# Turning quantised activations by DMA instead of on TensorE, in a fused sequence layer

## The chip, the cores and the metric

The kernel runs on one core of a Trainium2 chip. The metric is the device time of one execution in microseconds (us); lower is better. The engines are named as in the profile: PE (TensorE) with its weight loads PEld, DVE (VectorE), ACT (ScalarE), POOL (GpSimd) and SP (SyncE), which only issues DMAs. Each engine runs its own instructions in order and waits for others through semaphores.

## The reference, cut to what matters

The input x has 8 sequences of 512 rows of 256 values.

```
v      = x @ W_write.T
reads  = chunked decaying linear attention of x over itself, values v
x1     = layernorm(x + x + alpha * (reads @ W_read.T))
xq     = fp4(x1)                       # blocks of 16 along the row
gate   = xq @ fp4(w_gate).T            # 704 columns
up     = xq @ fp4(w_up).T
h      = silu(gate) * up
out    = layernorm(x1 + fp4(h) @ fp4(w_down).T)

fp4(a): scale = max(|block|) / 6 (at least 1e-12); a / scale is rounded to the
        grid 0, 0.5, 1, 1.5, 2, 3, 4, 6 with its sign, and multiplied by scale
```

## The kernel before, in words

The work is cut by sequence n (0 to 7), each of four tiles of 128 rows. Tiles of the second part are numbered k = 4n + t, 0 to 31. Buffers of two parities serve k, and pairs of tiles u = 0, 1 serve x. The 512 scores of a sequence are computed directly (the recurrence is folded into a decay mask). Float32 products are made of float32r parts: every operand is split into a rounded part (`_hi`) and a remainder (`_lo`), and a product is three matmuls (hi hi, hi lo, lo hi; `split_matmuls` L1709, `late_matmuls` L1719).

For a sequence: `scores` and `values` on PE from the transposed x; `decay_scores` on DVE (L1135); `reads` on PE; `x_residual` on DVE (L1159); the layernorm on ACT, DVE and POOL. Then x is quantised in pairs of tiles: maxima, scales and reciprocals on DVE; `x_normalise` on POOL (L390); squares on ACT (L680, into `x_sq`, bfloat16 in SBUF); `magic_add` (L1094) and `to_grid` (L1099) on DVE, which round to the grid by adding a large number; and `x_dequant` on POOL (L398), which multiplies the grid by its scale. PE transposes the result (`xq_transpose`, L1783), ACT rounds it (L688) and DVE takes the remainder (L1200).

For a tile k: `gate_up` on PE (512 + 512 + 384 columns, 18 matmuls) into three PSUM banks; silu on ACT (L699); the product on DVE (L1209); the same quantising of the 704 columns of h (L1215, L1083, L1084, L1089, L406, L703, L1094, L1099, L413); six transposes on PE (`h_transpose`, L1817), since the 704 columns are padded to 768 by repeating the last 64 (L712); rounding on ACT (L719) and the remainder on DVE in two parts (L1236); 17 matmuls of `down` (L1821); residual (L1245), deviations (L723) and layernorm (L731).

The four weights' parts in six pieces w are quantised the same way in the first 60 us and transposed by PE in nine fills.

The order on each engine is written out by hand as lists of calls: a prologue, a loop body of four tiles run three times, and an epilogue. Each call carries in its last argument the semaphores that say when its PSUM bank is free. SP loads x, x transposed and the weights, and stores 32 tiles of the output, in one list.

Of the kernel before, what the change touches and what calls it, by code (L numbers as in the profile page):

```python
# [5 lines left out]
F32 = mybir.dt.float32  # L31
F32R = mybir.dt.float32r
# [20 lines left out]
def mk_seq_postln_kernel(nc, x_rows, xt_rows, w_attn, w_ffn, scalars, out):  # L53
# [12 lines left out]
    PAIR = 2 * D  # L66
    WU = 6
# [4 lines left out]
    with ExitStack() as ctx:  # L72
# [3 lines left out]
        def sem(name):  # L76
# [36 lines left out]
        z_off = sb("z_off", [P, TILES, D], BF16)  # L113
# [7 lines left out]
        x_ns = sb("x_ns", [P, 2, 2 * XB + 2])  # L121
        x_rs = sb("x_rs", [P, 2, 2 * XB])
        x_n = sb("x_n", [P, 2, PAIR])
        x_sq = sb("x_sq", [P, 2, PAIR], BF16)
        x_y = sb("x_y", [P, 2, PAIR])
        x_g = sb("x_g", [P, 2, PAIR])
        x_q = sb("x_q", [P, TILES, D])
        xqT_hi = sb("xqT_hi", [P, DK, T], F32R)
        xqT_lo = sb("xqT_lo", [P, DK, T], F32R)
# [3 lines left out]
        h_am = sb("h_am", [P, 2, HB // 4, 5])  # L133
        h_sc = sb("h_sc", [P, 2, HB])
        h_ns = sb("h_ns", [P, 2, HB])
        h_rs = sb("h_rs", [P, 2, HB])
        h_n = sb("h_n", [P, 2, I])
        h_sq = sb("h_sq", [P, 2, I], BF16)
        h_y = sb("h_y", [P, 2, I])
        h_g = sb("h_g", [P, 2, I])  # L140
# [44 lines left out]
        v_left = sem("v_left")  # L185
# [3 lines left out]
        read_filled, z_ready, z_dev, z_var, z_rstd_ready, z_shift_ready = (  # L189
            sem("read_filled"), sem("z_ready"), sem("z_dev"), sem("z_var"), sem("z_rstd_ready"), sem("z_shift_ready"))  # L190
# [3 lines left out]
        xq_left = sem("xq_left")  # L194
        xqT_filled, xqT_hi_ready, xqT_lo_ready = sem("xqT_filled"), sem("xqT_hi_ready"), sem("xqT_lo_ready")
# [60 lines left out]
        def _(sp):  # L256
# [24 lines left out]

            load_x_transposed(1)
# [1832 lines left out]
```

## Time and profile before

| | |
|---|---|
| median of 3 runs | 324.37 us (324.2 to 324.91) |
| profiled execution, span | 322.5 us |
| time around the span, against the median | 1.9 us |
| PE busy | 314.5 us, 97% |
| PEld busy | 285.2 us, 88% |
| DVE busy | 293.0 us, 91% |
| POOL busy | 238.2 us, 74% |
| ACT busy | 213.2 us, 66% |
| DMA moved | 15.69 MB |

Busy time is the union of an engine's instructions. Matmuls overlap, so the mean of one instruction is its latency; how far apart they start is its cost. An instruction group's idle time stands only for the time just before it, with the engine that ended it.

### The profile page before, as it was taken

What the parts mean: (1) busy time and instruction counts of PE and PEld (TensorE: products, weight loads), DVE (VectorE), ACT (ScalarE), POOL (GpSimd) and SP (SyncE); (2) the same over time, 40 slices, a digit from 0 to 9 for tenths busy, and PEclk for the clock granted to TensorE, in tenths of its full rate; (3) what the DMA queues carried; (4) which work ended last, traced back from release to release, by engine and by line L of the source; (5) the groups of instructions that cost most, each with busy time, mean ns of one, the idle gap of its engine ahead of it and who ended that gap; (6) DMA issues with size and microseconds to landing.
All of it is one profiled execution on the core that took longest, in us unless ns stands there. A gap on an engine that the chain in (4) does not pass through costs nothing.

```text
span 322.5 us, 6519 instructions
## 1 busy us (share of the span) xinstructions
PE 314.5 (97%) x2067; PEld 285.2 (88%) x2067; DVE 293.0 (91%) x746; ACT 213.2 (66%) x521; POOL 238.2 (74%) x258
## 2 busy tenths in 40 slices
PE   7999999999999999999999999999999999999994
PEld 3999988989998998999989998898989889998983
DVE  4799789989899999899998999889999999999973
ACT  7769994767775647844784556766675555665664
POOL 1999898668696868676886768777779588368872
PEclk9999999999999999999999999999999999999999
DMA  6830301010010200320020200021000000001002
GB/s 227 302 125 9 132 0 67 1 66 2 1 67 16 84 16 0 100 82 3 16 83 17 83 17 3 33 65 35 1 18 17 16 18 17 19 16 35 17 33 84
DMA packets 8242, 15.69 MB, mean 49 GB/s; under 512 B 1040, under 2 KB 5136, under 8 KB 8208
## 3 DMA queue, kind: packets, MB, share of 16 engines
q1 hardware_dynamic: 7920, 15.01, 14.0%
q8 instruction: 17, 0.28, 0.4%
q10 hardware_dynamic: 288, 0.26, 0.3%
q14 instruction: 17, 0.14, 0.1%
HBM read 11.08 MB, written 4.19 MB: 47 GB/s over the span
## 4 chain that ended last, share of the span: by engine, by line
PE 69%; DVE 17%; issue 5%; ACT 4%; POOL 3%; ACTq 0%; DVEq 0%; POOLq 0%
PE gu L1712 11%; PE gu L1716 11%; PE gu L1713 11%; PE bank L1817 5%; PE bank L1712 4%; PE bank L1716 4%; PE bank L1713 4%; PE bank L1722 3%; DVE h_y L1094 3%; PE bank L1725 3%; PE bank L1726 3%; DVE w_raw L1209 2%; DVE hqT_lo L1236 2%; DVE h_am L1215 2%; PE bank L1783 2%
## 5 line engine op out<-in xcount | busy, mean ns | idle before, releaser
L413 POOL TENSOR_TENSOR h_q<-h_g,h_ns 128x704 f32<-128x704 f32 x32 | 51.2, 1604 | 47.7 <-DVE h_g L1099 47.6
L1712 PE MATMUL gu<-guT_hi,xqT_hi 128*128 128x512 f32 (+1 forms) x192 | 74.0, 386 | 0.7 <-DVE w_raw L1209 0.6
L1713 PE MATMUL gu<-guT_lo,xqT_hi 128*128 128x512 f32 (+1 forms) x192 | 72.2, 376 | 0.0
L1716 PE MATMUL gu<-guT_hi,xqT_lo 128*128 128x512 f32 (+1 forms) x192 | 56.6, 376 | 0.0
L699 ACT ACTIVATE w_raw<-gu 128x512 f32<-128x512 f32 x64 | 29.3, 462 | 32.7 <-PE gu L1716 32.4
L406 POOL TENSOR_TENSOR h_n<-w_raw,h_rs 128x704 f32<-128x704 f32 x32 | 47.0, 1472 | 3.4 <-DVE h_rs L1089 3.2
L719 ACT CAST hqT_hi<-bank 128x512 fp32r<-128x512 f32 x64 | 30.4, 478 | 17.7 <-PE bank L1817 17.2
L1712 PEld LDWEIGHTS gu<-guT_hi,xqT_hi 128*128 128x128 f32 x192 | 36.1, 188 | 6.0 <-ACT xqT_hi L688 0.9
L1716 PEld LDWEIGHTS gu<-guT_hi,xqT_lo 128*128 128x128 f32 x192 | 35.5, 188 | 6.0 <-ACT xqT_lo L693 0.2
L1713 PEld LDWEIGHTS gu<-guT_lo,xqT_hi 128*128 128x128 f32 x192 | 36.1, 188 | 4.8
L1094 DVE SCALAR_TENSOR_TENSOR h_y<-h_sq,h_n 128x704 f32<-128x704 bf16 x34 | 36.9, 1090 | 0.0
L1236 DVE TENSOR_TENSOR hqT_lo<-bank,hqT_hi 128x512 fp32r<-128x512 f32 x64 | 34.4, 542 | 1.9 <-ACT hqT_hi L719 1.8
L1209 DVE TENSOR_TENSOR w_raw<-w_raw,gu 128x512 f32<-128x512 f32 x64 | 32.4, 507 | 3.2 <-ACT w_raw L699 2.0
L1099 DVE SCALAR_TENSOR_TENSOR h_g<-h_sq,h_y 128x704 f32<-128x704 bf16 x34 | 32.4, 960 | 0.4
L368 POOL TENSOR_TENSOR pr_lo<-pr,pr_hi 128x512 fp32r<-128x512 f32 (+3 forms) x32 | 32.4, 1023 | 0.3 <-ACT pr_hi L658 0.3
L1817 PE MATMUL bank<-ident,h_q 128*128 128x128 f32 x192 | 30.4, 273 | 0.7 <-DVE wq_gu L1245 0.4
L1215 DVE TENSOR_REDUCE h_am<-w_raw 128x44 f32<-128x704 f32 x32 | 27.8, 868 | 0.3
L703 ACT ACTIVATE h_sq<-h_n 128x704 bf16<-128x704 f32 x32 | 25.4, 793 | 2.9 <-POOL h_n L406 2.9
L1817 PEld LDWEIGHTS bank<-ident,h_q 128*128 128x128 f32 x192 | 23.2, 140 | 4.5 <-issue 0.8
L398 POOL TENSOR_TENSOR x_q<-x_g,x_ns 128x512 f32<-128x512 f32 x16 | 18.3, 1142 | 11.7 <-DVE x_g L1099 11.7
L658 ACT CAST pr_hi<-pr 128x512 fp32r<-128x512 f32 (+3 forms) x32 | 14.7, 458 | 11.0 <-DVE pr L1135 10.9
L420 POOL TENSOR_TENSOR o_rstd<-o_ve,neg_half 128x1 f32<-128x1 f32 x31 | 19.5, 631 | 2.6 <-DVE o_ve L1252 2.6
(159 smaller groups left out, 936.7 us busy)
## 6 DMA issues: line engine op xcount, KB each, us to landing
xs<-in_x_rows_dram SPq DMA_DIRECT2D x8, 512.0 KB, 3.4
out_dram<-wq_gu SPq DMA_DIRECT2D x32, 128.0 KB, 1.7
x_full<-in_xt_rows_dram SPq DMA_DIRECT2D x7, 512.0 KB, 3.2
w_raw<-in_w_ffn_dram SPq DMA_DIRECT2D x6, 352.0 KB, 6.0
w_pair<-in_w_attn_dram SPq DMA_DIRECT2D x1, 512.0 KB, 5.2
x_full<-in_xt_rows_dram SPq DMA_DIRECT2D x1, 256.0 KB, 2.6
x_full<-in_xt_rows_dram ACTq DMA_DIRECT2D x1, 256.0 KB, 3.4
scal<-in_scalars_dram ACTq DMA_DIRECT2D x1, 1.0 KB, 1.7
```

The costliest lines, as they stand in the source:

```text
L368: nc.gpsimd.tensor_tensor(pr_lo[:, c], pr[:, c], pr_hi[:, c].bitcast(F32), ALU.subtract).then_inc(pr_lo_ready, 1)
L406: nc.gpsimd.tensor_tensor(blocks(h_n[:, p, :]), blocks(h[:, p, :]), per_block(h_rs[:, p, :], HB), ALU.mult).then_inc(h_norm, 1)
L413: nc.gpsimd.tensor_tensor(blocks(h_q[:, p, 0:I]), blocks(h_g[:, p, :]), per_block(h_ns[:, p, :], HB), ALU.mult).then_inc(h_quant, 1)
L1094: nc.vector.scalar_tensor_tensor(y, sq, MAGIC_C, v, ALU.add, ALU.add).then_inc(magic_sem, 1)
L1099: nc.vector.scalar_tensor_tensor(g, sq, MAGIC_C, y, ALU.add, ALU.subtract).then_inc(grid_sem, 1)
L1209: nc.vector.tensor_tensor(h[:, p, c], silu[:, p, c], up_of[half], ALU.mult).then_inc(h_ready, 1)
L1215: nc.vector.tensor_reduce(h_am[:, p, :, 0:4], blocks(h[:, p, :]), AX.X, ALU.max, apply_absolute_value=True).then_inc(h_amax, 1)
L1236: nc.vector.tensor_tensor(hqT_lo[:, p, c], h_bank[t][g][:, 0:c.stop - c.start], hqT_hi[:, p, c].bitcast(F32), ALU.subtract).then_inc(hT_lo ...
L1712: nc.tensor.matmul(dst, lh, rh, start=(first and i == 0), stop=False)
L1713: nc.tensor.matmul(dst, lh, rl, start=False, stop=False)
L1716: last = nc.tensor.matmul(dst, ll, rh, start=False, stop=(end and i == len(terms) - 1))
L1817: last = nc.tensor.transpose(h_bank[t][g][:, at - h_part[g].start:at - h_part[g].start + P], h_q[:, t % 2, at:at + P], ident[:])
```

## The change

The new kernel computes the same. Six things differ.

1. The grid of x and of h (multiples of a half up to 6) is written by `to_grid` as bfloat16 and turned by a transposing DMA from SBUF to SBUF (`turn_x_grid`, `turn_h_grid`). For h the repeated 64 columns are copied in the grid (`hg_repeat`).
2. The scales are transposed by PE in one instruction per tile of h or pair of x (`h_scale_rows`, `x_scale_rows`, 48 or 32 rows of 128), copied by ACT to SBUF, written to scratch in device memory by one DMA, and read back with every row repeated over the 16 partitions of its block (`spread_*`, 393 KB for h). So that the rows of one partition group lie together in scratch, `h_divisors` writes the scales in another order, with one more instruction; `x_divisors` does so in the same number.
3. POOL multiplies the turned grid by the spread scales (`x_spread`, `h_spread`) into a float32 tile that is already transposed. ACT rounds it in one instruction of 768 columns, and DVE takes the remainder in one, both from SBUF. Tiles 30 and 31 keep the old way.
4. The squares go to PSUM in float32, two banks for h and one for x. PSUM is one tensor of eight banks; banks 0 to 2 hold gate and up, and tables say for every step which of the other five it takes.
5. The mean is formed before the deviations, and POOL computes the variance (`x_stats`, `out_stats`). The remainders that PE made by subtraction for the first sequences (v, x) are taken by DVE.
6. All five lists are written in another order, without a loop. `gate_up` waits for the silu of the tile before to refill the gate bank, and for the product only for the others.

The core of the diff (the call lists are shown below by their instructions):

```diff
+            def spread_h_scales(k, p, turn):
+                sp.wait_ge(hs_written[p], 16 * turn)
+                if turn > 1:
+                    sp.wait_ge(h_quant, k - 1)
+                sp.dma_start(h_sT[:, p, :], over_rows(h_scales_dram[k])).then_inc(hs_landed[p], 16)
+
+            def turn_h_grid(k, p, turn):
+                sp.wait_ge(hg_repeated, k + 1)
+                if turn > 1:
+                    sp.wait_ge(h_quant, k - 1)
+                sp.dma_start_transpose(h_gT[:, p, :, :], h_g[:, p, :]).then_inc(hg_turned[p], 16)
...
+            def x_stats(n, u):
...
+                nc.gpsimd.tensor_scalar(z_ve[:, c], z_ssq[:, c], 1.0 / D, LN_EPS, ALU.mult, ALU.add).then_inc(z_var, 1)
...
+            def h_spread(k, p, turn):
+                pool.wait_ge(hs_landed[p], 16 * turn)
+                pool.wait_ge(hg_turned[p], 16 * turn)
+                if k >= 2:
+                    pool.wait_ge(hT_lo_ready, 2 * k - 2)
+                else:
+                    pool.wait_ge(wT_filled, FILLS)
+                nc.gpsimd.tensor_tensor(h_q[:, p, :], h_gT[:, p, :, :].rearrange("p c t -> p (c t)"), h_sT[:, p, :],
+                                        ALU.mult).then_inc(h_quant, 1)
...
-            def h_squares(k, p):
+            def h_squares(k, p, free):
                 act.wait_ge(h_norm, k + 1)
-                nc.scalar.activation(h_sq[:, p, :], h_n[:, p, :], ACT.Square, scale=ROOT_K).then_inc(h_square, 1)
+                wait_all(free)
+                nc.scalar.activation(two_banks(h_sq_at[k]), halves(h_n[:, p, :]), ACT.Square,
+                                     scale=ROOT_K).then_inc(h_square, 1)
...
+            def copy_h_scales(k, p, turn):
+                act.wait_ge(hs_filled, k + 1)
+                if turn > 1:
+                    act.wait_ge(hs_written[p], 16 * turn - 16)
+                nc.scalar.copy(h_s[:, p, :], ps[0:SROWS, hs_at[k], 0:P]).then_inc(hs_copied, 1)
+
+            def h_round_all(k, p):
+                if k >= 2:
+                    act.wait_ge(down_filled, k - 1)
+                act.wait_ge(h_quant, k + 1)
+                nc.scalar.copy(hqT_hi[:, p, :], h_q[:, p, :]).then_inc(hT_hi_ready, 2)
...
             def h_to_grid(k, p):
-                to_grid(h_g[:, p, :], h_sq[:, p, :], h_y[:, p, :], h_magic, h_grid, k + 1)
+                if k >= 2:
+                    if k < 32:
+                        dve.wait_ge(hg_turned[p], 16 * (k // 2))
+                    else:
+                        dve.wait_ge(h_quant, k - 1)
+                to_grid(halves(h_g[:, p, 0:I]), two_banks(h_sq_at[k]), halves(h_y[:, p, :]), h_magic, h_grid, k + 1)
...
+            def h_rest_all(k, p):
+
+                dve.wait_ge(hT_hi_ready, 2 * k + 2)
+                nc.vector.tensor_tensor(hqT_lo[:, p, :], h_q[:, p, :], hqT_hi[:, p, :].bitcast(F32),
+                                        ALU.subtract).then_inc(hT_lo_ready, 2)
...
-            def xq_transpose(n, u, free):
-                pe.wait_ge(x_quant, 2 * n + u + 1)
+            def x_scale_rows(n, u, free):
+                pe.wait_ge(x_div, 2 * n + u + 1)
                 wait_all(free)
-                for dk in range(DK):
-                    for q in range(2):
-                        at = dk * 2 * P + q * P
-                        last = nc.tensor.matmul(xq_bank[u][:, at:at + P], x_q[:, 2 * u + q, dk * P:(dk + 1) * P], ident[:],
-                                                is_transpose=True, start=(dk == 0 and q == 0),
-                                                stop=(dk == DK - 1 and q == 1))
-                last.then_inc(xqT_filled, 1)
...
+            def h_scale_rows(k, p, free):
+                pe.wait_ge(h_div, k + 1)
+                wait_all(free)
+                nc.tensor.transpose(ps[0:SROWS, hs_at[k], 0:P], h_ns[:, p, :], ident[:]).then_inc(hs_filled, 1)
...
+        h_sq_at = ((3, 4), (3, 4), (6, 7), (5, 6), (5, 6), (5, 6), (5, 6), (3, 4), (3, 4), (4, 5), (3, 4), (5, 6), (5, 6),
```

On PE, in the middle of the program before, between the values of a sequence and the `down` of a tile (`xqT` and `hqT` are the turned operands, `dnT` the down weights):

```order
L1713 MATMUL bank<-comb_lo,xT_hi 128x256
L1716 MATMUL bank<-comb_hi,xT_lo 128x256 x2
L1783 MATMUL bank<-ident,x_q 128x128 x4
L1817 MATMUL bank<-ident,h_q 128x128 x4
L1827 MATMUL gu<-dnT_hi,hqT_hi 128x256
```

And on PE in the new program, between a gate and the `down` of a tile:

```order
L2227 MATMUL ps<-guT_lo,xqT_hi 128x512
L2230 MATMUL ps<-guT_hi,xqT_lo 128x512 x2
L2321 MATMUL ps<-ident,h_ns 48x128
L2329 MATMUL ps<-dnT_hi,hqT_hi 128x256
L2226 MATMUL ps<-dnT_hi,hqT_hi 128x256
```

The transposes of x (4 per pair) and h (6 per tile) are gone, and one of the scales stands in their place.

On SP, in the middle of the program before, where loads and stores alternate (`xs` is x by rows, `wq_gu` the output buffer):

```order
L279 DMA out_dram<-wq_gu 128x256 x3
L271 DMA x_full<-in_xt_rows_dram 128x1024
L279 DMA out_dram<-wq_gu 128x256
L275 DMA xs<-in_x_rows_dram 128x1024
L279 DMA out_dram<-wq_gu 128x256 x2
```

And on SP in the new program, around the stores of tiles 2 and 3:

```order
L314 DMA h_scales_dram<-h_s 48x128
L342 DMA_TRANSPOSE x_gT<-x_g 128x4x128
L320 DMA h_sT<-h_scales_dram 128x1x768
L309 DMA out_dram<-wq_gu 128x256
L326 DMA_TRANSPOSE h_gT<-h_g 128x6x128 x2
L314 DMA h_scales_dram<-h_s 48x128 x2
L309 DMA out_dram<-wq_gu 128x256
L330 DMA x_scales_dram<-x_s 32x128
L320 DMA h_sT<-h_scales_dram 128x1x768 x2
```

Between two stores there are now writes and reads of scales and transposing DMAs, each behind its own wait.

On DVE near the start before, from the residual of sequence 1 to the first grid of x (`h_sc` and `h_rs` belong to the weights here):

```order
L1159 SCALAR_TENSOR_TENSOR x,z_sum<-xs,bank 128x256 x2
L1089 RECIPROCAL h_rs<-h_sc 128x44
L1135 TENSOR_TENSOR pr<-gu,mask 128x512
L1094 SCALAR_TENSOR_TENSOR x_y<-x_sq,x_n 128x512
L1099 SCALAR_TENSOR_TENSOR x_g<-x_sq,x_y 128x512
```

And on DVE in the new program, from the third weight's rounding to the same grid of x:

```order
L1478 SCALAR_TENSOR_TENSOR h_y<-ps,h_n 128x704
L1541 SCALAR_TENSOR_TENSOR x,z_sum<-xs,ps 128x256 x2
L1483 SCALAR_TENSOR_TENSOR h_g<-ps,h_y 128x704
L1549 TENSOR_SCALAR z_nm<-z_sum 128x1 x2
L1519 TENSOR_TENSOR pr<-ps,mask 128x384
L1478 SCALAR_TENSOR_TENSOR x_y<-ps,x_n 128x512
L1483 SCALAR_TENSOR_TENSOR x_g<-ps,x_y 128x512
```

The first grid of x now stands directly behind the third weight's, ahead of the fourth weight's and of the scores of sequence 2.

## Rows read from the trace of the kernel before

**Rows 1.** The page: span, then busy us, share of the span, instructions.
```profile
span 322.5 us, 6519 instructions
...
PE 314.5 (97%) x2067; PEld 285.2 (88%) x2067; DVE 293.0 (91%) x746; ACT 213.2 (66%) x521; POOL 238.2 (74%) x258
```

**Rows 2.** Windows, first and last: us, PE, PEld, DVE, ACT, POOL busy, clock, DMA.
```profile
0.00:20.00 20.00, 18.27 (x101) 13.84 (x102) 14.03 (x36) 14.04 (x26) 12.93 (x19) 1.00 0.63 216
...
310.00:322.50 12.50, 7.70 (x63) 7.13 (x61) 6.13 (x24) 6.28 (x18) 4.77 (x10) 1.00 0.20 63
```

**Rows 3.** Timeline of PE in mid-program: start us, us, then the instruction.
```profile
156.67 0.60 PE L1783 MATMUL bank<-ident,x_q 128*128 128x128 f32 x4
157.10 0.60 PE L1817 MATMUL bank<-ident,h_q 128*128 128x128 f32 x4
157.46 0.37 PE L1827 MATMUL gu<-dnT_hi,hqT_hi 128*128 128x256 f32 x1
```

**Rows 4.** Groups by form on PE: busy us, mean ns, idle before.
```profile
L1817 PE MATMUL bank<-ident,h_q 128*128 128x128 f32 x192 | 30.4, 273 | 0.7 <-DVE wq_gu L1245 0.4 <-DVE hqT_lo L1236 0.2
...
L1750 PE MATMUL bank<-v_hi,neg_ident 128*128 128x512 f32 x4 | 1.7, 457 | 0.0
```

**Rows 5.** Groups by form on DVE.
```profile
L1094 DVE SCALAR_TENSOR_TENSOR h_y<-h_sq,h_n 128x704 f32<-128x704 bf16 x34 | 36.9, 1090 | 0.0
L1099 DVE SCALAR_TENSOR_TENSOR h_g<-h_sq,h_y 128x704 f32<-128x704 bf16 x34 | 32.4, 960 | 0.4
...
L1236 DVE TENSOR_TENSOR hqT_lo<-bank,hqT_hi 128x512 fp32r<-128x512 f32 x32 | 21.5, 671 | 1.4 <-ACT hqT_hi L719 1.4
...
L1094 DVE SCALAR_TENSOR_TENSOR x_y<-x_sq,x_n 128x512 f32<-128x512 bf16 x16 | 15.7, 981 | 0.8 <-ACT x_sq L680 0.8
L1236 DVE TENSOR_TENSOR hqT_lo<-bank,hqT_hi 128x256 fp32r<-128x256 f32 x32 | 13.2, 413 | 0.6 <-ACT hqT_hi L719 0.4
...
L1143 DVE TENSOR_TENSOR v_lo<-bank,v_hi 128x512 fp32r<-128x512 f32 x12 | 8.1, 673 | 0.5 <-ACT v_hi L646 0.3
...
L1083 DVE TENSOR_SCALAR h_ns<-h_am 128x44 f32<-128x44 f32 x38 | 7.0, 185 | 0.6
...
L1252 DVE TENSOR_SCALAR o_ve<-o_ssq 128x1 f32<-128x1 f32 x32 | 4.5, 141 | 0.0
...
L1094 DVE SCALAR_TENSOR_TENSOR h_y<-gu,h_n 128x704 f32<-128x704 f32 x4 | 3.5, 886 | 0.7 <-ACT gu L615 0.6
L1099 DVE SCALAR_TENSOR_TENSOR h_g<-gu,h_y 128x704 f32<-128x704 f32 x4 | 3.5, 870 | 0.0
```

**Rows 6.** Groups by form on POOL.
```profile
L413 POOL TENSOR_TENSOR h_q<-h_g,h_ns 128x704 f32<-128x704 f32 x32 | 51.2, 1604 | 47.7 <-DVE h_g L1099 47.6
...
L398 POOL TENSOR_TENSOR x_q<-x_g,x_ns 128x512 f32<-128x512 f32 x16 | 18.3, 1142 | 11.7 <-DVE x_g L1099 11.7
...
L422 POOL TENSOR_TENSOR o_shift<-o_nm,o_rstd 128x1 f32<-128x1 f32 x31 | 6.0, 193 | 2.4
```

**Rows 7.** DMA: queue (packets, MB, share of 16 engines); issues (KB each, us to landing).
```profile
q1 hardware_dynamic: 7920, 15.01, 14.0%
...
xs<-in_x_rows_dram SPq DMA_DIRECT2D x8, 512.0 KB, 3.4
out_dram<-wq_gu SPq DMA_DIRECT2D x32, 128.0 KB, 1.7
```

**Rows 8.** Timeline of PE: scores of sequence 2, first gate matmul.
```profile
33.55 0.71 PE L1722 MATMUL gu<-xT_hi 128*128 128x512 f32 x2
...
40.52 0.39 PE L1712 MATMUL gu<-guT_hi,xqT_hi 128*128 128x512 f32 x1
```

**Rows 9.** Timeline of DVE: the third weight's grid, the first grid of x.
```profile
24.50 0.89 DVE L1099 SCALAR_TENSOR_TENSOR h_g<-gu,h_y 128x704 f32<-128x704 f32 x1
...
36.64 0.69 DVE L1099 SCALAR_TENSOR_TENSOR x_g<-x_sq,x_y 128x512 f32<-128x512 bf16 x1
```

**Rows 10.** Groups by form on ACT.
```profile
L688 ACT CAST xqT_hi<-bank 128x512 fp32r<-128x512 f32 x16 | 9.4, 586 | 10.0 <-PE bank L1783 9.9
```

More of the change, by code:

```diff
@@ L1546, in _ @@
[L1546 to L1561 removed]
+            out_residual(15, 3)
@@ new lines, in _ @@
+            values(3, 1, [(h_grid, 5)])
+            scores(3, 2, [(hs_copied, 5)])
+            reads(3, 0, [(hs_copied, 4)])
+            scores(3, 3, [(z_ready, 6)])
+            x_scale_rows(2, 1, [(pr_ready, 15)])
+            h_scale_rows(5, 1, [(wT_lo_ready, 9)])
+            gate_up(8, 2, 0, 0)
+            h_scale_rows(6, 0, [(hs_copied, 6)])
+            pe.wait_ge(wT_lo_ready, 9)
+            down(0, 0, [(xs_copied, 6)])
+            gate_up(8, 2, 0, 1)
+            down(1, 1, [(x_grid, 6)])
@@ new lines, in _ @@
+            x_scale_rows(3, 0, [(hs_copied, 7)])
+            gate_up(9, 2, 1, 0)
+            reads(3, 1, [(o_ready, 1)])
+            gate_up(9, 2, 1, 1)
+            gate_up(10, 2, 2, 0)
+            scores(4, 0, [(h_grid, 7)])
+            scores(4, 1, [(h_grid, 7)])
+            values(4, 0, [(o_ready, 2)])
+            gate_up(10, 2, 2, 1)
+            x_scale_rows(3, 1, [(pr_ready, 18)])
+            gate_up(11, 2, 3, 0)
+            h_scale_rows(7, 1, [(h_grid, 9)])
+            down(2, 2, [(h_grid, 9)])
@@ new lines, in _ @@
+            gate_up(11, 2, 3, 1)
+            values(4, 1, [(x_grid, 8)])
+            gate_up(12, 3, 0, 0)
+            reads(4, 0, [(v_lo_ready, 10)])
+            down(3, 3, [(h_grid, 10)])
+            scores(4, 2, [(z_ready, 9)])
+            h_scale_rows(8, 0, [(h_grid, 10)])
+            scores(4, 3, [(o_ready, 4)])
+            h_scale_rows(9, 1, [(pr_ready, 19)])
+            down(4, 0, [(o_ready, 3)])
+            h_scale_rows(10, 0, [(pr_ready, 20)])
+            down(5, 1, [(pr_ready, 17)])
@@ new lines, in _ @@
+            x_scale_rows(4, 0, [(hs_copied, 10)])
+            gate_up(12, 3, 0, 1)
+            gate_up(13, 3, 1, 0)
+            reads(4, 1, [(h_grid, 11)])
+            gate_up(13, 3, 1, 1)
+            gate_up(14, 3, 2, 0)
+            values(5, 0, [(z_ready, 10)])
+            down(6, 2, [(h_grid, 11)])
+            x_scale_rows(4, 1, [(xs_copied, 9)])
+            gate_up(14, 3, 2, 1)
+            gate_up(15, 3, 3, 0)
+            h_scale_rows(11, 1, [(xs_copied, 10)])
+            scores(5, 0, [(v_lo_ready, 11)])
@@ new lines, in _ @@
+            gate_up(15, 3, 3, 1)
+            scores(5, 1, [(hs_copied, 12)])
+            gate_up(16, 4, 0, 0)
+            reads(5, 0, [(pr_ready, 22)])
+            gate_up(16, 4, 0, 1)
+            down(7, 3, [(z_ready, 11)])
+            scores(5, 2, [(h_grid, 14)])
+            scores(5, 3, [(h_grid, 14)])
+            values(5, 1, [(o_ready, 8)])
+            h_scale_rows(12, 0, [(pr_ready, 24)])
+            h_scale_rows(13, 1, [(pr_ready, 23)])
+            down(8, 0, [(h_grid, 13)])
+            x_scale_rows(5, 0, [(v_lo_ready, 12)])
@@ L2083 @@
+            down(31, 3, [(hT_lo_ready, 64)])
 def kernel(**inputs):
```

2500 lines of the change are left out of this document (1469 added, 1031 removed).

## The prediction

> **What bounds the kernel now.** I read the busy shares first: TensorE (PE) works 314.5 of 322.5 us, VectorE (DVE) 293.0, GpSimd (POOL) 238.2 [rows 1]. The windows tell where the missing 8.0 us of PE are: the first 20 us have 18.3 busy and the last 12.5 us have 7.7, so 6.5 of the 8.0 are start and end, at a granted clock of 1.00, the 2.4 GHz level, in both [rows 2]. In between PE is idle for 1.5 us. A busy PE need not be a necessary PE, so I looked at how densely its instructions start: eight 128-column transposes, four of x and four of h, take from 156.67 to 157.46, 0.79 us, 0.099 us each [rows 3]. They are packed; their mean of 273 ns is latency [rows 4]. PE is the bound by throughput. DVE is second: of its 29.5 idle us, 6.0 lie in the first window and 6.4 in the last [rows 2], so in the middle it has 17 us to spare. That is all the room the change has before DVE takes over.
>
> **The change part by part.** The profiled execution has a span of 322.5 us; the median of the runs is 324.37, so 1.9 us lie around the span, and I add them at the end.
>
> *PE.* Thirty of 32 h tiles lose six transposes each and 16 pairs of x tiles lose four: 180 + 64 = 244 at 0.099 = 24.2 us. Six subtracting matmuls of 512 columns go too (four of v, two of x). Their mean is 457 ns [rows 4], latency again; between 0.099 and 0.457 each I take 0.23, the middle, 1.4 us. The new scale transposes are 30 + 16 = 46. They move the same 128 columns of the identity, so 0.099 each, 4.6 us. Net: 24.2 + 1.4 - 4.6 = 21.0 us less, PE 293.5. All of it counts, since PE has no cover.
>
> *DVE.* Rows are [rows 5]. The squares are read from PSUM in float32 where they were bfloat16 in SBUF. Both forms are in the trace: h_y 1090 against 886 ns, h_g 960 against 870, thirty-four each: -6.9 and -3.1 us. For x_y there is only the old form, 981; the nearest 512-column operation with one PSUM input is v_lo, 673: 16 x 0.308 = -4.9. The remainder of h was two reads of PSUM, 671 + 413 ns, 32 times (34.7 us); it becomes one of 768 columns with both inputs in SBUF. No row has it. By the h_g row with two SBUF inputs, 960 x 768/704 = 1047 ns; by the h_y row 1189; by the PSUM form 949. I take 1047: 31.4 + 2.2 for the two tiles left = 33.6, -1.1 (ends -4.0 and +3.2). Four v remainders and two x remainders come over from PE: 6 x 0.673 = +4.0. Each of 30 tiles gets a third scale instruction, 185 ns: +5.6. The variance moves to POOL: 32 x 0.141 = -4.5; that of x I leave at zero, since its two halves are now two mean instructions. Sum -10.9, DVE 282.1, between 279 and 286. DVE then has 20 us idle in 302, of which 12 are again start and end. So the cover in the middle shrinks from 17 to about 8 us.
>
> *POOL and ACT.* The spreading multiply of h goes over 768 elements instead of 704: 1604 x 768/704 = 1750 ns, 30 x 0.146 = +4.4 us; the variances are 48 small instructions at 193 ns, +9.3 [rows 6]. POOL is 252, 83% of the new span: covered. ACT gets 46 small copies and loses some remainders; it is the least busy and I price it at nothing. If its cover went, the copies would delay the scale writes, which the turns wait for only through the multiply.
>
> *The DMA queue.* This is what no row of before shows. SP issued plain loads and stores; now it issues 46 writes of scales, 46 spreads and 46 transposing DMAs between them. SP is in order: behind a spread that waits for its write stand the next turns, loads and stores, and behind those POOL's multiply, the remainder, and down. A 128 KB store lands in 1.7 us, a 512 KB load in 3.4 [rows 7]. A write and its spread thus cost SP at least 1.7 us of waiting, 46 x 1.7 = 78 us in all, which a span of 300 holds. The turn of one h tile is 196 KB. Lower end: the store, 1.7 us. Upper end: if it goes in pieces of 256 bytes it has 768 packets; the old queue's 7920 packets took 14.0% of 16 engines' 322.5 us, 91 ns each [rows 7], so 768 x 91 / 16 = 4.4 us, plus a landing of 1.7, 6.1 us. I take 3.4, the 512 KB load, nearest to the middle. In the steady part that hides: h_gT and h_q have two buffers, so a turn has two tiles' time, 2 x 9.4 us, for 3.4 of DMA and 1.75 of POOL, and in DVE's order the remainder of a tile comes three to four tiles behind its grid.
>
> For the transfer the Trainium skill has two rules that disagree. Its page Advanced Engine Details and Errata, section X-Bar Transpose (TRN2), says that transposing DMAs run as fast as ordinary ones, which would put the turn near the lower end. Its page VectorE: DVE Perf Modes, section The three transpose paths, gives 1309 ns for a 128x128 block; with 244 blocks in one queue that would be 319 us of turns, more than the span, and by it the change would lose. No run here shows either yet; the rival below works such a case out from rows.
>
> *The start.* This is where latency is not covered. Before, PE began the scores of sequence 2 at 33.55 and the first gate matmul at 40.52 [rows 8]. The scores and the first values of sequence 2 and the transposes of x now stand behind it, and of that stretch about 1.3 us of weight work (eight transposes at 0.099, two subtractions at 0.23) stays in front, less 1.0 of dropped subtractions before it: PE arrives at about 34. The x grid was written from 36.64 to 37.3 [rows 9]. In DVE's new order it stands before the later weights' and the scores' work; behind the third weight's grid, which was ready near 25.4 [rows 9], I estimate some 6 us of DVE work up to it (four rounding passes, maxima and scales of two more weights), ending near 31.5. Then come the turn T, 1.14 us on POOL [rows 6] and a rounding of 0.6 on ACT [rows 10]: 33.2 + T. With T of 1.7, 3.4 or 6.1 the first gate matmul starts at 34.9, 36.6 or 39.3. I take 36.6, so 2.6 us of new idle on PE.
>
> *Sum.* 293.5 of work, 8.0 of the old idle, 2.6 at the start: a span of 304.1, and 1.9 around it: 306.0 us. The last two tiles keep the old path over PE, so the end stays as it was.
>
> **The rivals.**
> *A, waits eat part of it.* With DVE at 282 and PE at 293, each has little to spare, and PE waits for PSUM banks that the squares now occupy from ACT's write until DVE's second read. For it: five shared banks serve all but gate and up, and the DVE margin halves. Against it: in the old trace PE waited only 1.5 us in the middle at a similar ratio of the two engines (0.93, now 0.96). If the middle costs PE 12 us more, the time is 318.
>
> *B, the turns fill the queue (the other side).* All turns go through one queue, one behind another. There are 244 blocks of 128x128, from about 31 us to some 15 us before the end. The old time leaves 322.5 - 46 = 277 us for them, so the change is slower from 277/244 = 1.13 us a block. At the packet price above a block is 128 x 91/16 = 0.73 us, 178 us in all: not a bound. At twice that, if the read of a piece and its write do not overlap, it is 1.46: 356 + 46 + 1.9 = 404 us; at a landing of 1.7 a block 463. For it: small pieces were the old queue's dear ones and nothing shows them overlapping. Against it: it takes more than 1.5 times the price of the packets in the trace.
>
> *C, more than forecast.* Fewer DVE instructions with two SBUF inputs may shorten POOL's, and deeper lag may close the old 1.5 us in the middle; with no new wait at the start the time is 293.5 + 6.5 + 1.9 = 302, and with DVE's lower end perhaps 299.
>
> *D, nothing moves.* Only by chance: A at 20 us more, 324 to 326.
>
> **How the numbers follow.** The forecast with its own range of 301 to 312: 0.56. C, 297 to 301: 0.10. A, 312 to 322: 0.18. D: 0.02. B: 0.14. A measurement of this kernel can tell about 0.2%, 0.65 us, from no change. Faster: 0.56 + 0.10 + 0.18 = 0.84; same 0.02 (D); slower 0.14 (B). The range runs from 298 to 320, which leaves out B, D, the top of A and the bottom of C, together about 0.2.
>
> **What would show it.** PE busy near 293 and matmuls still packed; idle of 2 to 3 us before the first gate matmul, with the x grid's turn as releaser; h_y at about 0.89 us and the 768-column remainder near 1.05; the turn landing in 2 to 6 us; DVE about 282. The forecast is wrong if the turns land later than 9 us after issue, if SP waits for them rather than for its semaphores, or if PE shows over 10 us of idle in the middle. Then A or B holds, told apart by who releases: DVE for A, the queue for B.

## The result and the profile after

The changed kernel takes 350.33 us (median of 4 runs, 349.44 to 352.72) against 324.34 us before (4 runs): ratio 1.081, 95% interval [1.077, 1.085]. The forecast was 306.0 us with a range of 298 to 320, and 0.14 for slower. It was wrong in sign.

Times are medians of all executions of a kernel, while the ratios leave out slower ones; three kernels below had one such execution, and without it their medians are 337.15 us (for 338.44), 330.18 (for 331.41) and 320.17 (for 320.81).

The page of the changed kernel, to be held against [rows 1]: busy time by engine, granted clock in 40 slices, and the chain that ended last.
```profile
span 347.4 us, 6525 instructions
...
PE 303.9 (87%) x1863; PEld 265.9 (77%) x1863; DVE 309.9 (89%) x720; ACT 222.6 (64%) x531; POOL 252.3 (73%) x306
...
PEclk9999899999999999999999998999999999998998
...
q1 hardware_dynamic: 49568, 40.01, 48.7%
...
DVE 38%; issue 18%; POOL 18%; PE 13%; ACT 7%; DMA 4%; SPq 1%; DVEq 0%; ACTq 0%; POOLq 0%
```
PE was busy 314.5 of 322.5 us; now it is idle for 43.5 us of 347.4. The work did leave PE (204 instructions fewer), but DVE, forecast at 282 us, stands at 309.9 with 26 instructions fewer than before. The largest share of the last chain, 38%, is DVE's.

What PE waited for (line, releaser: us in total, times, longest), the four largest:
```profile
PE ps L2287 <- DVE x_sc L1567: 7.0, 8, 2.3
PE ps L2226 <- DVE pr L1519: 3.4, 1, 3.4
PE ps L2236 <- DVE h_g L1483: 3.1, 6, 1.2
PE ps L2329 <- DVE wq_gu L1660: 2.8, 2, 1.5
```
Of PE's 43.5 idle us DVE ended 30.7, all rows of this view taken together; no row names a transfer. L2287 is the new transpose of x's scales: the prediction gave such transposes 0.099 us each and no wait.

Groups by form on DVE after the change, to be held against [rows 5]: busy us, mean ns of one, idle before.
```profile
L1483 DVE SCALAR_TENSOR_TENSOR h_g<-ps,h_y 128x704 bf16<-128x704 f32 x38 | 33.6, 886 | 2.7 <-DMA h_gT<-h_g 0.7 <-DVE h_y L1478 0.5
L1478 DVE SCALAR_TENSOR_TENSOR h_y<-ps,h_n 128x704 f32<-128x704 f32 x38 | 33.2, 873 | 0.8 <-ACT ps L965 0.4 <-ACT ps L879 0.2
L1651 DVE TENSOR_TENSOR hqT_lo<-h_q,hqT_hi 128x768 fp32r<-128x768 f32 x30 | 32.3, 1084 | 0.2 <-ACT hqT_hi L998 0.2
L1621 DVE TENSOR_SCALAR h_ns<-h_am 128x8 f32<-128x8 f32 x30 | 16.0, 533 | 0.2 <-issue 0.2
...
L1584 DVE TENSOR_TENSOR xqT_lo<-x_q,xqT_hi 128x512 fp32r<-128x512 f32 x16 | 12.5, 780 | 0.2 <-ACT xqT_hi L954 0.2
...
L1478 DVE SCALAR_TENSOR_TENSOR x_y<-ps,x_n 128x512 f32<-128x512 f32 x16 | 10.9, 682 | 0.8 <-ACT ps L941 0.8
...
L1565 DVE TENSOR_SCALAR x_ns<-x_am 128x32 f32<-128x32 f32 x16 | 7.8, 490 | 1.0
L1624 DVE TENSOR_SCALAR h_sc<-h_am 128x44 f32<-128x44 f32 x30 | 7.7, 258 | 0.0
L1619 DVE TENSOR_SCALAR h_ns<-h_am 128x40 f32<-128x40 f32 x30 | 6.6, 220 | 1.2
L1467 DVE TENSOR_SCALAR h_ns<-h_am 128x44 f32<-128x44 f32 x8 | 5.2, 646 | 0.3
```
Most of the big instructions came as priced. The odd row is the smallest: h_ns over 8 elements takes 533 ns, more than twice the 220 ns of its neighbour over 40. A view by tile gives it 157 ns at least, 365 in the middle and 1629 at most, where h_ns of before ran from 139 to 201. An instruction of 8 elements that takes 0.16 to 1.6 us is waiting for something while it counts as busy. Of the 29 that the timeline shows singly, 15 take over 0.25 us, and 14 of these end within 0.12 us of the end of a POOL instruction; the 6 that start with POOL idle take 0.17 us.

One such place, in a timeline of DVE and POOL (start us, length us), and what PE does after it:
```profile
203.65 1.05 POOL L592 TENSOR_TENSOR x_n<-x,x_rs 128x512 f32<-128x512 f32 x1
203.81 0.24 DVE L1619 TENSOR_SCALAR h_ns<-h_am 128x40 f32<-128x40 f32 x1
203.92 0.82 DVE L1621 TENSOR_SCALAR h_ns<-h_am 128x8 f32<-128x8 f32 x1
204.64 1.73 DVE L1624 TENSOR_SCALAR h_sc<-h_am 128x44 f32<-128x44 f32 x1
204.66 1.66 POOL L629 TENSOR_TENSOR h_q<-h_gT,h_sT 128x768 f32<-128x768 bf16 x1
206.40 0.43 DVE L1473 RECIPROCAL h_rs<-h_sc 128x44 f32<-128x44 f32 x1
...
208.49 0.88 DVE L1519 TENSOR_TENSOR pr<-ps,mask 128x384 f32<-128x384 f32 x2
```
```profile
204.08 0.28 PE L2239 MATMUL ps<-xT_lo,xT_hi 128*128 128x256 f32 x1
204.20 0.28 PE L2240 MATMUL ps<-xT_hi,xT_lo 128*128 128x256 f32 x1
...
205.25 0.51 PE L2230 MATMUL ps<-guT_hi,xqT_lo 128*128 128x384 f32 x2
209.18 0.55 PE L2226 MATMUL ps<-comb_hi,xT_hi 128*128 128x256 f32 x1 [3.42 <-DVE pr L1519]
209.53 0.42 PE L2227 MATMUL ps<-comb_lo,xT_hi 128*128 128x256 f32 x1
209.75 0.42 PE L2226 MATMUL ps<-comb_hi,xT_hi 128*128 128x256 f32 x1
209.96 0.41 PE L2227 MATMUL ps<-comb_lo,xT_hi 128*128 128x256 f32 x1
```
h_ns starts at 203.92 and ends at 204.74, when POOL's x_n ends (204.70). h_sc starts at 204.64, POOL's h_q beside it at 204.66; both end at 206.3 to 206.4. DVE lost 2.2 us on 52 elements, pr came late by that, and PE stood still for 3.42 us. After that its matmuls of 256 columns start 0.21 us apart, where the two at 204.08 are 0.12 apart: the granted clock is at 1.2 GHz for a while, as two windows show (columns as in [rows 2]):
```profile
203.00:205.00 2.00, 2.00 (x15) 2.00 (x14) 1.89 (x4) 0.22 (x2) 2.00 (x3) 1.00 0.70 117
...
209.50:211.00 1.50, 1.50 (x8) 1.50 (x8) 1.29 (x5) 1.50 (x5) 1.50 (x2) 0.50 0.83 193
```
So this wait on DVE is paid for twice. The clock's row on the page shows four such dips, the digits 8.

### The profile page after: what moved, and what is told of

The parts are those of the page before. It is cut to its first block, busy times and chain, and to the rows that moved or that the text cites. A ratio compares the mean times of both kernels' runs of the same rounds, so it can differ in the third digit from the quotient of the medians.

```text
span 347.4 us, 6525 instructions
## 1 busy us (share of the span) xinstructions
PE 303.9 (87%) x1863; PEld 265.9 (77%) x1863; DVE 309.9 (89%) x720; ACT 222.6 (64%) x531; POOL 252.3 (73%) x306
## 4 chain that ended last, share of the span: by engine, by line
DVE 38%; issue 18%; POOL 18%; PE 13%; ACT 7%; DMA 4%; SPq 1%; DVEq 0%; ACTq 0%; POOLq 0%
DVE h_y L1478 4%; POOL h_q L629 4%; DVE w_raw L1594 3%; DVE hqT_lo L1651 3%; DVE h_am L1602 3%; PE ps L2226 3%; PE ps L2227 3%; PE ps L2230 3%; DVE h_g L1483 3%; POOL o_rstd L640 2%; DMA h_sT<-h_scales_dram 2%; DVE x_am L1556 2%; DVE h_ns L1621 2%; DVE x_ns L1565 2%; POOL pr_lo L568 2%
## 5 line engine op out<-in xcount | busy, mean ns | idle before, releaser
L2226 PE MATMUL ps<-guT_hi,xqT_hi 128*128 128x512 f32 (+1 forms) x192 | 74.0, 386 | 4.0 <-DVE w_raw L1594 2.1
L2227 PE MATMUL ps<-guT_lo,xqT_hi 128*128 128x512 f32 (+1 forms) x192 | 72.3, 376 | 0.0
L629 POOL TENSOR_TENSOR h_q<-h_gT,h_sT 128x768 f32<-128x768 bf16 x30 | 51.0, 1701 | 18.0 <-DVE hqT_lo L1651 13.1
L2230 PE MATMUL ps<-guT_hi,xqT_lo 128*128 128x512 f32 (+1 forms) x192 | 56.8, 377 | 0.5 <-DVE xqT_lo L1584 0.5
L2226 PEld LDWEIGHTS ps<-guT_hi,xqT_hi 128*128 128x128 f32 x192 | 36.6, 190 | 10.9 <-DVE w_raw L1594 4.0
L2230 PEld LDWEIGHTS ps<-guT_hi,xqT_lo 128*128 128x128 f32 x192 | 35.7, 189 | 6.5 <-DVE xqT_lo L1584 1.3
L2226 PE MATMUL ps<-dnT_hi,hqT_hi 128*128 128x256 f32 x160 | 40.1, 285 | 0.0
L2227 PE MATMUL ps<-dnT_lo,hqT_hi 128*128 128x256 f32 x160 | 40.1, 285 | 0.0
L2227 PEld LDWEIGHTS ps<-guT_lo,xqT_hi 128*128 128x128 f32 x192 | 36.5, 190 | 4.2
L1483 DVE SCALAR_TENSOR_TENSOR h_g<-ps,h_y 128x704 bf16<-128x704 f32 x38 | 33.6, 886 | 2.7 <-DMA h_gT<-h_g 0.7
L1651 DVE TENSOR_TENSOR hqT_lo<-h_q,hqT_hi 128x768 fp32r<-128x768 f32 x30 | 32.3, 1084 | 0.2 <-ACT hqT_hi L998 0.2
L2227 PEld LDWEIGHTS ps<-dnT_lo,hqT_hi 128*128 128x128 f32 x160 | 30.8, 193 | 0.0
```

The costliest lines, as they stand in the source:

```text
L629: nc.gpsimd.tensor_tensor(h_q[:, p, :], h_gT[:, p, :, :].rearrange("p c t -> p (c t)"), h_sT[:, p, :], ALU.mult).then_inc(h_quant, 1)
L1483: nc.vector.scalar_tensor_tensor(g, sq, MAGIC_C, y, ALU.add, ALU.subtract).then_inc(grid_sem, 1)
L1651: nc.vector.tensor_tensor(hqT_lo[:, p, :], h_q[:, p, :], hqT_hi[:, p, :].bitcast(F32), ALU.subtract).then_inc(hT_lo_ready, 2)
L2226: nc.tensor.matmul(dst, lh, rh, start=(first and i == 0), stop=False)
L2227: nc.tensor.matmul(dst, lh, rl, start=False, stop=False)
L2230: last = nc.tensor.matmul(dst, ll, rh, start=False, stop=(end and i == len(terms) - 1))
```

## The experiments

All kernels were compared with the kernel before on the same chip; its median there was 324.3 to 324.5 us. Ratios have a 95% interval.

**Odd outer dimensions.** The theory (P): a TENSOR_SCALAR whose outer dimension is even waits for POOL's running instruction. The kernel before kept h's maxima as 11 groups of 4; the changed kernel keeps them as 22 groups of 2 (so that the scales can be turned), and writes the last chunk's four twice. The edit, shortened, with remarks behind the #:
```
-  h_sc = sb("h_sc", [P, 2, HB])              # 44 = 22 x 2
+  h_sc = sb("h_sc", [P, 2, HB + 2])          # 46 = 23 x 2
-  rest.unsqueeze(1).to_broadcast((P, 2, 2, 2))
+  rest.unsqueeze(1).to_broadcast((P, 3, 2, 2))   # written three times
   x_ns: one instruction over 4 x 4 x 2 -> two, over 3 x 4 x 2 and 5 x 2
```


> The changed kernel (350.3 us) with the shapes of DVE's small scale instructions made odd in their outermost dimension, and nothing else: 23 rows where there were 22, 3 repeats where there were 2, and the 4-row instruction of x cut into one of 3 and one of 5 rows. Theory P (shape): in the changed kernel the instructions whose outermost dimension is even take 490 to 646 ns on average (up to 1.7 us) where the odd ones take about 185 to 220, because an even one takes a second SBUF port and waits for POOL's instruction to end; DVE work falls from 309.9 to about 285 us, those means to about 190, and, since DVE is on the chain that ends last, the time to about 325 us (between 318 and 335). Theory Q (the DMA path): the time is lost to the turns, spreads and SP's order; the small instructions become short or not, but the time stays above 342.

Measured 336.77 us, ratio 1.037 [1.036, 1.039]: 13.6 us back. That is below Q's 342 and 1.8 us above P's range: the shapes are a cause, and not the only one. DVE fell from 309.9 to 290.2 us. The scale instructions of this kernel, by form:
```profile
L1623 DVE TENSOR_SCALAR h_ns<-h_am 128x40 f32<-128x40 f32 x30 | 6.6, 220 | 1.2
L1628 DVE TENSOR_SCALAR h_sc<-h_am 128x46 f32<-128x46 f32 x30 | 5.8, 192 | 0.2 <-issue 0.2
L1625 DVE TENSOR_SCALAR h_ns<-h_am 128x12 f32<-128x12 f32 x30 | 4.9, 165 | 0.0
L1566 DVE TENSOR_SCALAR x_ns<-x_am 128x24 f32<-128x24 f32 x16 | 3.1, 194 | 1.0
```
More elements and less time: 12 elements in 165 ns where 8 took 533.

**The same in the kernel before.** h_am as 22 x 2 and h_sc as 44, nothing else:

> The kernel before (324.3 us) with one thing of the change: the block maxima of w and h laid out as 22 rows of 2 (even) instead of 11 rows of 4. The same 44 maxima, the same instructions in the same order. Theory P: the h_ns instruction grows from 185 ns to 500 to 650 ns, with maxima above 1.2 us; DVE busy rises by about 12 us, and the time by 3 to 10 us, less than the sum because DVE had 17 us to spare in the middle. Theory Q and anybody who holds the layout for indifferent: 324 us, within 0.3%.

333.98 us, ratio 1.029 [1.028, 1.031], within P's range. The layout alone costs the kernel before 9.6 us. h_ns went from 185 ns [rows 5] to 533; x_ns (17 x 2) stayed:
```profile
L1083 DVE TENSOR_SCALAR h_ns<-h_am 128x44 f32<-128x44 f32 x38 | 20.3, 533 | 0.6
...
L1084 DVE TENSOR_SCALAR h_sc<-h_am 128x44 f32<-128x44 f32 x38 | 11.3, 299 | 0.0
L1083 DVE TENSOR_SCALAR x_ns<-x_am 128x34 f32<-128x34 f32 x16 | 2.9, 179 | 0.5
```

**An odd count that is equal on both sides.** The means of x, 2 columns read and 2 written, took 552 ns in the kernel before. They were laid out as 3 and 3.

> The kernel before with its 2-column mean and variance of x laid out as 3 columns (the third is unused), so that no outer dimension is even. Theory P (a DVE instruction with an even outer dimension waits for POOL's running instruction): z_nm goes from 552 to about 150 ns, 6 us less on DVE, and the time stays within 1 us or falls by up to 2 us, since PE binds there. Rival (552 ns is a property of the tiny shape): z_nm stays near 550 ns and the time at 324.4 us.

324.71 us, ratio 1.001 [1.000, 1.002]; no gain, and the instruction kept its wait:
```profile
L1174 DVE TENSOR_SCALAR z_nm<-z_sum 128x3 f32<-128x3 f32 x16 | 8.9, 554 | 0.8 <-ACT z_off L677 0.7
```
The theory had said that odd is enough, and this row refutes that form of it. The rival (552 ns belong to the tiny shape) forecast the same two numbers, but it does not fit the single instructions: in this kernel and in the one before, the 4 z_nm that start with POOL idle take 0.16 to 0.17 us, and 9 of the 10 over 0.25 us end with a POOL instruction. z_ve, of the same form, took 157 ns; it stands directly behind z_nm, which has waited by then.

What fits all rows: outer counts of source and destination that are both even wait (22 and 44 in h_sc, 16 and 4 in x_ns), and so do 3 and 3; 11 and 44, 23 and 46, 17 and 34, 20 and 5 (h_ns over 40) and 12 and 3 (x_ns over 24) do not, nor do 1 and 1. In this count neighbouring dimensions that are evenly spaced are one, which is an inference from the code; without it several pairs that do not wait would be odd and equal (11 and 11, 23 and 23, 5 and 5). The Trainium skill has the rule in this form, on its page Advanced Engine Details and Errata, section VectorE Performance Modes: the two-port mode wants source and destination in SBUF and outer dimensions both even, or both odd (above 1) and equal, and two-port instructions and GpSimd's block each other. The traces agree, and add the size: up to the whole length of POOL's instruction, 1.7 us here.

**Squares back in SBUF.** On the odd-shaped kernel, the squares of w, h and x as bfloat16 tiles in SBUF, and PE's waits for the banks they had held dropped:

> e1_odd with the squares of w, h and x back in SBUF as bfloat16, and PE's waits for banks that only the squares held dropped; same order, same turns. Theory W1 (the banks that squares occupy until DVE's second read make PE wait): PE's waits for h_g and x_g go, DVE gains 34 x 0.2 + 34 x 0.09 + 16 x 0.3 = 15 us of work, and the time falls to 328 to 334 us. Rival W2 (DVE's work and its order bind, the banks only show it): DVE's 15 us come back, 340 to 350 us.

384.34 us, ratio 1.188 [1.183, 1.193]: 48 us slower, far beyond W2's 340 to 350. PE's waits for h_g and x_g, which free the squares' banks, were 9.4 us in the odd-shaped kernel and are gone here; with the squares in PSUM the kernel avoids something much worse. So this run prices the way out, and does not show that the banks cost nothing. It also makes ACT's squares of x wait for the turn, since they share x_g's tile. On DVE:
```profile
L1493 DVE SCALAR_TENSOR_TENSOR h_g<-h_sq,h_y 128x704 bf16<-128x704 bf16 x38 | 51.1, 1348 | 1.6
L1488 DVE SCALAR_TENSOR_TENSOR h_y<-h_sq,h_n 128x704 f32<-128x704 bf16 x38 | 47.1, 1241 | 1.0 <-ACT h_sq L974 0.7
```
With one PSUM input they take 886 and 873 ns, with two SBUF inputs beside a busy POOL 1348 and 1241; POOL itself rose from 252 to 290 us. In the kernel before h_y took 1090 in the same form [rows 5]. Read singly, the h_g here that start with POOL idle take 0.89 us on average and those that start beside it 1.47; for h_y of before it is 0.88 and 1.53.

**Without the transfers.** Turned tiles and spread scales replaced by constant tiles on the changed and on the odd-shaped kernel; left out: all transposing DMAs, writes and spreads. In the first two the fills of the constants on POOL held DVE's constants back by about 4 us (its even-shaped instructions waited for them), so they start late; the third has the fills moved.

> The changed kernel without its 46 turns, 46 writes and 46 spreads: POOL multiplies constant tiles instead, as soon as the scales are copied and the grid is there, so this leaves out the transposition of x and h and their scales, and it takes all latency and queueing of these DMAs out. Every instruction of PE, DVE, ACT and POOL stays, in its order. Theory Q: the time falls to 310 us or less, near the forecast. Theory P: the DMA path costs little on the chain (POOL's waits for landings are 5 us in all), so the time falls by less than 8 us, to 343 or more.

> Both edits together: odd shapes and no turns, writes and spreads (it leaves out the transposition of x and h and their scales). What is left above 306 us is then due neither to the ports nor to the DMAs, but to the order of the instructions, the PSUM banks and true work. If P and Q add, it falls by the sum of both; theory P expects 315 to 325, theory Q 303 to 310. A result above 325 says that a third cause, the order or the banks, carries most of the loss.

> e4_odd_no_dma again, with the four fills of constant tiles on POOL moved behind its first wait for DVE's constants, so that they no longer hold the start back. Left out as there: the transposing DMAs, the writes and the spreads of scales (output differs). Compared with e1_odd, 336.77 us. Theory W (what is left of the loss is waiting between PE and DVE over PSUM banks and in-order queues): 331 to 334 us, since the queue carries 3 to 6 us. Rival Q (the latency of the turns is what the remaining 30 us are made of): below 322 us.

349.12 us (1.074 [1.068, 1.080]), 333.52 us (1.026 [1.023, 1.029]) and 327.96 us (1.012 [1.010, 1.013]). The last is the clean one: of the odd-shaped kernel's 336.8 us the transfers carry 8.8, more than the 3 to 6 that W had allowed, and the time is 3 us below W's range. The first is above P's 343 as expected, the second missed P's 315 to 325. Rival Q is out: 22 us above the forecast remain with no transfer at all.

**Turns kept, spreads gone:**

> e1_odd without the writes and spreads of scales, with the transposing DMAs kept (scales are a constant 1, so the output differs). e1_odd takes 336.8 us and without all three 328.0. If the transposing DMAs carry the difference of 9 us: 335 to 337 us. If the spreads (384 KB for h) do, by their own landing time and by the queue they fill: 328 to 331 us.

329.13 us, ratio 1.015 [1.012, 1.017]. The 46 turns cost some 1.2 us (329.1 - 328.0, no more than either kernel scatters by), the writes and spreads 7.6 (336.8 - 329.1). One queue carries all; the issues of SP in the odd-shaped kernel, and a POOL instruction that waited for a spread:
```profile
75.78 0.60 SPq L336 DMA_DIRECT2D x_sT<-x_scales_dram  x1
76.43 0.58 SPq L320 DMA_DIRECT2D h_sT<-h_scales_dram  x1
...
83.15 1.67 POOL L629 TENSOR_TENSOR h_q<-h_gT,h_sT 128x768 f32<-128x768 bf16 x1 [1.64 <-DMA h_sT<-h_scales_dram]
```
A spread of 384 KB, issued at 76.43, released POOL at 83.1, 6.7 us later. Without the spreads a turn lands in 2.7 us in the median and a store in 1.7; with them 3.2 and 2.1.

**Less work on DVE, less on PE.** Two probes on the odd-shaped kernel: h's remainder over 256 of 768 columns; and down without 160 of its products.

> e1_odd with the remainder of h formed over 256 of 768 columns from the third tile on (the other columns stay as they were, so the output differs): takes about 28 x 0.7 = 20 us off DVE and nothing off PE. If DVE binds through its sum of work (W2): 318 to 326 us. If order and banks bind (W1) or the turns do (Q): 332 to 336 us.

> e1_odd without the 160 products of h's remainder in five of the six chunks (output differs): takes 160 x 0.107 = 17 us off PE (256 columns at 2.4 GHz) and nothing off DVE. If PE's throughput still sets the pace as in the kernel before: 318 to 321 us. If DVE binds (W2): 333 to 337 us. If PE and DVE wait for each other in turn (W1): 326 to 331 us.

332.63 us (1.027 [1.023, 1.031]) and 338.44 us (1.041 [1.036, 1.046]). Some 11 us of busy time less on DVE (290.2 to 278.8) gave 4.1 us; 13 us less on PE (302.7 to 289.7) gave nothing, with PE's mean granted clock down from 0.982 to 0.968. The first lies where W1 and Q had it and outside W2; the second is above all three of its ranges, nearest to W2's. With the lighter remainder POOL's busy time fell as well, from 252.3 to 243.9. Neither sum binds. What is left is who waits for whom, and the written order would set that; the next runs change it.

**Another order.** The same instructions as in the odd-shaped kernel, calls moved on each engine and banks chosen anew, by a search over orders with durations from the traces. A piece of DVE's order, at the left in the odd-shaped kernel, at the right in the last and best of the orders below:
```
-  h_to_grid(12, 0)            +  h_magic_add(11, 1)
-  v_rest(5, 0)                +  out_residual(6, 2)
-  out_residual(6, 2)          +  decay_scores(5, 3)
-  out_mean(6, 0)              +  h_to_grid(11, 1)
-  h_rest_all(8, 0)            +  hidden(13, 1, 1)
```


> e1_odd with the same instructions in another order: the calls on each engine moved, and the PSUM banks of the short fills chosen anew, by a search over orders that used the durations which e1_odd's trace showed. Nothing is computed otherwise. Theory O (what is left of the loss is that the written order does not fit the real durations and the latencies of turns and spreads; each engine has room): 322 to 328 us. Rival Q (turns, spreads and shared work cost this whatever the order): 334 to 338 us.

355.93 us, ratio 1.095 [1.089, 1.102]: 19 us worse, both expectations missed. The search had taken every landing as fixed; its order bunched the transfers. DVE waited 16.0 us for turns and POOL 16.5 for spreads, and the same transfers landed later (KB, median us):
```profile
out_dram<-wq_gu SPq DMA_DIRECT2D x32, 128.0 KB, 3.6
...
h_scales_dram<-h_s SPq DMA_DIRECT2D x30, 24.0 KB, 3.7
h_gT<-h_g SPq DMA_TRANSPOSE x30, 4.9
```
In the odd-shaped kernel these three stood at 2.1, 1.7 and 3.2. So landings behind one another, and idle PE, were put into it:

> As r1_odd_reordered (same instructions as e1_odd, another order), but the search now knew two things that the traces of e1_odd and r1_odd_reordered showed: transfers of SP's queue land one behind the other (a spread of h's scales holds the ones behind it by about 2.6 us), and TensorE's clock falls to half after a stretch in which it idled. Durations are the longer of those in the two traces. Theory O' (the written order does not fit the transfers' landings and leaves PE idle in clumps; an order that does brings most of the forecast back): 318 to 325 us. Rival S (each tile's chain of waits costs it in any order): 333 us or more.

325.47 us, ratio 1.006 [1.002, 1.010]: 11.3 us back, half a us above the range of O'. Then the changed kernel itself, even shapes and all, in this order, and the light remainder again:

> The changed kernel with its own instructions, even outer dimensions as it has them, in the order and banks of r2_odd_reordered; nothing else differs from the changed kernel. If order and shapes are two separate losses that add: 350.3 - 11.3 = 339 us, and 13.6 above r2_odd_reordered (325.5). If the fitted order also hides the waits for POOL: 326 to 333 us. If the order helps only the odd shapes: 346 us or more.

> r2_odd_reordered with h's remainder over 256 of 768 columns from the third tile on (output differs): about 20 us off DVE, as in e7_odd_light_rest, where that gave 4.1 us. If DVE's sum of work binds once the order fits (it is 93 to 96% busy in the middle): 308 to 315 us. If the chain of waits binds in this order too: 321 to 325 us.

338.22 us (1.042 [1.040, 1.045]) and 320.21 us (0.989 [0.988, 0.991]). The order, with the banks that go with it, gives the changed kernel 12.1 us, and shapes and order add, as the first expectation had it: 338.2 - 325.5 = 12.7 where they cost 13.6 before. The lighter remainder lies between its two expectations: 12.2 us less on DVE (290.1 to 277.9) gave 5.3 us, so DVE's sum did not bind alone in that order. Two more orders:

> r2_odd_reordered without the 63 one-column means on DVE: ACT squares the deviation times the column count from the sum (as the kernel before did), POOL scales the variance and forms the shift from the sum; the order searched again. Takes 64 x 0.145 = 9 us off DVE and a wait of ACT for DVE from each tile. If DVE binds in this order: 318 to 322 us, below both kernels. If not: 324 to 326 us, as r2_odd_reordered.

> The instructions of e1_odd and r2_odd_reordered once more in another order, searched for with durations and landings varied around those of the traces, so that it doesn't hang on one set of them. If what is left is an order's waiting: 318 to 322 us, below the kernel before. If each tile's chain of waits sets it: 324 to 328 us, as r2_odd_reordered.

The first missed: 331.41 us, 1.021 [1.017, 1.025]. DVE had 5.5 us less (290.1 to 284.6), POOL 7.7 more (259.8 to 267.5), its one-column shifts with a scalar from memory at 268 ns in the median for 191 in the form before. The second held: **320.81 us, 0.986 [0.982, 0.991], 1.4% below the kernel before.** It is the best of three searched orders. Part of its middle (columns as in [rows 2]):
```profile
260.00:300.00 40.00, 38.23 (x247) 34.89 (x246) 39.00 (x99) 27.86 (x68) 34.72 (x41) 1.00 0.64 143
```
There DVE is busy 39.0 of 40 us, and from 100 to 300 us it is never below 38.4; but PE stands at 38.2 to 39.8 in the same windows. Both are nearly full, and no run lightened either in this order, so which of them binds is not shown. The kernel before was not searched in this way, so this is no proof that the change beats its best order.

## Why the prediction was wrong

**The step that failed** is in DVE's sum: "Each of 30 tiles gets a third scale instruction, 185 ns: +5.6." The scale instructions of h and x (h_ns, h_sc, x_ns) had 7.0 + 7.1 + 2.8 us before and have 27.8 + 10.1 + 7.8 after: +28.8 where 5.6 were forecast. The step took the duration of a row for a property of its size, when it was one of its shape: 44 elements at 185 ns waited for nobody, 8 elements in an even layout wait for POOL. It costs 12.7 to 13.6 us of time. The prediction drew on the Trainium skill's page Advanced Engine Details and Errata for the turn alone, and did not weigh its section VectorE Performance Modes, which has the rule.

**The second failed step** is the cover: "the cover in the middle shrinks from 17 to about 8 us", as if margin were a store from which waits are paid. The odd-shaped kernel has DVE at 290 and PE at 303 in 335 us, 44 and 32 us of idle, and is still 30.8 us above the forecast; the order gives 16.0 of it back (336.8 to 320.8). Rival A had the mechanism and the releaser, DVE; its 12 us were too few by more than half, and it had no price for the clock. Its reason, banks held by squares, was a part: PE's waits for h_g and x_g are 7.4 us in the changed kernel, 9.4 in the odd-shaped one and 0.2 in the best order. The searched orders chose calls and banks together, so what each gave is not separated.

**The rest, by step.**
- PE's work: 293.5 forecast; 296.8 in the best order, 299.1 without transfers, 303.9 as it came, with stretches at 1.2 GHz inside. At its best 3.3 us more than forecast, 10.4 as it came.
- h_y, h_g, x_y: 873, 886 and 682 ns, forecast 886, 870 and 673. Right. The x remainder, priced at 673 for two more of them, went from 681 to 780 ns for all sixteen once both inputs lay in SBUF.
- The 768-column remainder: 1084 ns for 1047, right as it came, but not a constant: 1153 with odd shapes and 1301 in the best order, since it too has two SBUF inputs and POOL works beside it more of the time. In the best order that is 30 x 0.25 = 7.6 us of DVE over the forecast.
- POOL: 252.3 for 252.
- The turn: 2.8 us in the median for the 3.4 taken, SP busy 1.24 us with issuing one. Rival B, "slower from 1.13 us a block", is refuted: all 46 turns cost some 1.2 us. Its 91 ns a packet was a mean over mostly larger packets; those of 256 bytes took 33 ns on average in the odd-shaped kernel. The Trainium skill's 1309 ns a block (VectorE: DVE Perf Modes, The three transpose paths) is not what this trace shows, where six blocks land in 2.8 us; its page Advanced Engine Details and Errata, section X-Bar Transpose (TRN2), which has them as fast as ordinary transfers, agrees better: a 128 KB store landed in 1.9 us here and 512 KB loads in 4.2 to 5.1. The 319 us of turns that the prediction works out are less than the old span of 322.5, and more than the 277 that rival B allows.
- The spreads were given no price but the 1.7 us of SP before them. They cost 7.6 us.
- The moments of x, left at zero, gave something: 8.8 + 2.5 us of DVE before, 3.3 after.
- DVE's idle time, 20 us in 302, leaves out the new wait at the start: of the forecast's own span of 304.1 it is 22, and the cover 10 for 8.
- The start: the first gate matmul at 38.50, forecast 36.6. It waited for guT_lo of ACT, a weight, and not for the turn of x; with odd shapes it stood at 35.81.

Sum: 306.0 forecast + 13.6 shapes + 7.6 spreads + 1.2 turns + 22.0 with no transfer at all = 350.4. The 22.0 are the remainder and no measurement of one cause. Of all but the first of these losses the order takes back 16.0. The 14.8 us between the best order and the forecast are located and not explained: in its profile PE works 3.3 us more than forecast and is idle for 21.6 us where the forecast had 10.6; in the first 20 us alone it is idle for 5.6 us, where the kernel before had 1.7 [rows 2].

## What to carry to other kernels

Price a small instruction by its row only if its layout stays; where the outer dimensions of source and destination in SBUF become both even, or odd and equal, or where both inputs move to SBUF, add waits up to the length of GpSimd's instructions. A tell is a group whose longest is many times its shortest. When work leaves an engine that was 97% busy in a hand-fitted order, expect the gain only after the order has been fitted again, as here, with the queue of transfers as a part of that fit.

## What the runs showed that was not expected

- Large DVE instructions meet POOL on the SBUF side alone: with one operand in PSUM a 704-column instruction takes 873 to 886 ns, POOL busy or not; with both in SBUF it takes 0.88 us with POOL idle and 1.3 to 1.5 on average beside it, and POOL is slowed as well (252 to 290 us).
- How long a transfer of SP's queue takes depends on what was issued before it: a scale write of 24 KB lands in 1.7 us in one order and 3.7 in another, a turn in 2.7 us without spreads and 4.9 where they bunch. Orders made as if each landed behind the one before it, with a price for idle PE, came out at 325.5 and 320.8 us, one made with fixed landings and without it at 355.9.
- Idle PE costs its clock: after 3.42 us of idle the matmuls ran at half rate. The mean granted clock was 0.958 in the worst order, 0.989 in the best and 1.00 before.
- Orders of the same instructions, banks chosen with them, differ by 35 us (320.8 to 355.9).
